# The upper diagonal blocks of the first attention pass: mask by a bf16 matmul in the bank, four block maxima in one VectorE operation

## The reference

```python
content = einsum('bqhd,bkhd->bhqk', q + u_bias, k)
pos_score = _rel_shift(einsum('bqhd,khd->bhqk', q + v_bias, p))
attn = softmax((content + pos_score) / sqrt(128), axis=-1)
x = x + (attn @ v) @ Wo + bo
# router: layernorm, hidden layer, top 2 of 8 experts
for e in range(8):
    output += expert_mask[e] * ((x1 * gelu(x2)) @ W2[e] + b2[e])   # x1, x2 = split(x @ W1[e])
```

## Time and profile before

| | |
|---|---|
| median of 3 runs | 1679.14 us (1678.62 to 1680.92) |
| span of the profiled execution | 1679.0 us |
| loop over batches, about | 87 to 1232 us of the span |
| expert phase, about | 1313 us to the end |
| TensorE matmul busy, all | 1548.0 us, 92% |
| VectorE busy, all | 1397.8 us, 83% |
| ScalarE busy, all | 1108.9 us, 66% |
| GpSimd busy, all | 1103.0 us, 66% |

### The profile page before, as it was taken

The page is one execution under the profiler, slowest core; times in us unless marked ns, Lnnn a source line. Parts: engine busy times, 40 slices in busy tenths (PEclk is TensorE's granted clock), DMA queues, the critical chain, the costliest instruction groups (busy, mean ns, idle before and its releaser), DMA issues. The chain is left out here.

```text
span 1679.0 us, 50905 instructions
## 1 busy us (share of the span) xinstructions
PE 1548.0 (92%) x12492; PEld 1204.6 (72%) x12493; DVE 1397.8 (83%) x5262; ACT 1108.9 (66%) x2295; POOL 1103.0 (66%) x2088
## 2 busy tenths in 40 slices
PE   3789999999999999999999999999952699999997
PEld 1567776677777767777777776776741699999997
DVE  4669899989989987998998899899864588887886
ACT  2157777776777776677777777767730477777775
POOL 5247767767766775777677677667673276666665
PEclk8679999999999998999999999999985799999999
DMA  5746535535644553464365355346454244444443
GB/s 136 198 116 174 148 93 152 164 96 128 180 116 128 161 148 84 110 203 110 104 174 148 93 141 164 97 129 179 122 153 136 42 58 54 56 56 52 56 53 49
DMA packets 133844, 199.72 MB, mean 119 GB/s; under 512 B 20888, under 2 KB 95016, under 8 KB 133632
## 3 DMA queue, kind: packets, MB, share of 16 engines
q1 hardware_dynamic: 108064, 177.07, 39.0%
q0 software_dynamic: 25568, 20.14, 8.2%
HBM read 108.10 MB, written 75.20 MB: 109 GB/s over the span
## 5 line engine op out<-in xcount | busy, mean ns | idle before, releaser
L1084 DVE CUSTOM_DVE_ANT_0 junk<-pA,lmask 128x512 bf16<-128x512 f32 x1056 | 686.9, 683 | 65.1 <-PE pA L671 45.9
L986 ACT ACTIVATE prob<-pB 128x512 f32<-128x512 f32 x384 | 229.8, 598 | 205.5 <-PE pB L690 115.9
L1578 POOL DMA_INDIRECT out<-yb,dst x142 | 230.4, 1622 | 131.3 <-ACT yb L1656 78.5
L692 PE MATMUL pB<-QL,K 97*128 97x512 f32 (+3 forms) x768 | 286.4, 373 | 1.4 <-ACT upper_diag L986 1.2
L669 PE MATMUL pA<-K,QL 96*128 96x512 f32 (+3 forms) x792 | 282.1, 357 | 5.1 <-DMA K<-split_operands 3.4
L690 PE MATMUL pB<-QU,K 97*128 97x512 f32 (+3 forms) x640 | 267.5, 418 | 0.2
L671 PE MATMUL pA<-K,QU 96*128 96x512 f32 (+3 forms) x660 | 233.1, 354 | 4.4 <-DVE acc L1084 3.2
L988 ACT ACTIVATE prob<-pB 128x512 f32<-128x512 f32 x384 | 227.9, 594 | 12.7 <-PE pB L692 3.4
L708 PE MATMUL pC<-prob,vext 128*17 128x256 f32 x3088 | 217.8, 385 | 0.1
L576 POOL TENSOR_TENSOR prob<-prob,upper_diag 128x128 f32<-128x128 f32 x384 | 179.7, 468 | 31.9
L690 PEld LDWEIGHTS pB<-QU,K 97*128 97x128 f32 x640 | 122.0, 191 | 99.9 <-issue 62.3
(11 more groups left out here) (305 smaller groups left out, 3642.9 us busy)
## 6 DMA issues: line engine op xcount, KB each, us to landing
QL<-split_operands SPq DMA_DIRECT2D x67, 256.0 KB
QU<-split_operands SPq DMA_DIRECT2D x67, 256.0 KB
K<-split_operands SPq DMA_DIRECT2D x67, 256.0 KB
xg<-routed_rows SPq DMA_DIRECT2D x75, 132.0 KB
split_operands<-c_h SPq DMA_DIRECT2D x36, 256.0 KB, 6.1
split_operands<-c_l SPq DMA_DIRECT2D x36, 256.0 KB, 6.4
QL<-split_operands SPq DMA_DIRECT2D x67, 128.0 KB
QU<-split_operands SPq DMA_DIRECT2D x67, 128.0 KB
```

What stands on the lines that cost most here:

```text
L692: mm = pe.matmul(pB[:, q0 + up:q0 + HALF], K[0:r, s, k], QL[0:r, s, q0 + up:q0 + HALF], start=True, stop=True)
L986: act.activation(p[:, 0:HALF], pB[:, 0:HALF], ACT.Exp, scale=SCALE).then_inc(p_exp, 1)
L1084: v.tensor_tensor_reduce(out, src[:, :], lmask[:, at:at + HALF], 1.0, -3.0e38, ALU.add, ALU.max, acc[:, s, qb, n % 2:n % 2 + 1]).then_inc( ...
L1578: po.indirect_dma_start(dram["out"], bass.IndirectOffsetOnAxis(dst[k][:, a:a + 1], 0), yb[k][:, a, :], None, compute_op=ALU.add).then_inc( ...
```

## The change

The mask of the upper diagonal pieces goes into the bank by one more matmul, ahead of the four: bf16 identity (stationary) times the bf16 mask, read four times by a stride of 0, 512 columns. The four score matmuls then add to the bank (`start=False`). VectorE takes the four block maxima with one `tensor_reduce` over 128 x 4 x 128. `umask` becomes bf16, and GpSimd sets up a bf16 identity `ident_b` (one memset and one select more). The registers of GpSimd in the expert phase are loaded with the runtime check of their bounds, which was skipped before.

```diff
-        lmask, umask = sb("lmask", [P, 15 * P], BF16), sb("umask", [P, P])
+        lmask, umask, ident_b = sb("lmask", [P, 15 * P], BF16), sb("umask", [P, P], BF16), sb("ident_b", [P, P], BF16)
-        DVE_SET, DVE_BIAS, POOL_SET = 13, 11, 15
+        DVE_SET, DVE_BIAS, POOL_SET = 13, 11, 17
             po.memset(umask[:, :], 0.0).then_inc(set_pool, 1)
+            po.memset(ident_b[:, :], 0.0).then_inc(set_pool, 1)
...
-            po.wait_ge(set_pool, 9)
+            po.wait_ge(set_pool, 10)
             po.affine_select(out=ident[:, :], in_=ident[:, :], compare_op=ALU.not_equal, fill=1.0, base=0,
                              pattern=[[-1, P]], channel_multiplier=1).then_inc(set_pool, 1)
+
+            po.affine_select(out=ident_b[:, :], in_=ident_b[:, :], compare_op=ALU.not_equal, fill=1.0, base=0,
+                             pattern=[[-1, P]], channel_multiplier=1).then_inc(set_pool, 1)
...
                 else:
+                    pe.matmul(dst[:, :].rearrange("p (n k) -> p n k", k=P), ident_b[:, :], umask[:, :].unsqueeze(1).to_broadcast([P, 4, P]),
+                              start=True, stop=False, skip_group_check=True)
                     for i in range(4):
                         q = slice(P * (4 * (n % 2) + i), P * (4 * (n % 2) + i) + P)
-                        mm = pe.matmul(dst[:, P * i:P * i + P], QU[0:KROWS, s, q], K[0:KROWS, s, q], start=True, stop=True)
+                        mm = pe.matmul(dst[:, P * i:P * i + P], QU[0:KROWS, s, q], K[0:KROWS, s, q], start=False, stop=True, skip_group_check=True)
...
                     g = n % 2
-                    for i in range(4):
-                        blk = 4 * g + i
-                        ttr = v.tensor_tensor_reduce(out[:, P * i:P * i + P], src[:, P * i:P * i + P], umask[:, :], 1.0, -3.0e38, ALU.add, ALU.max,
-                                                     acc[:, s, blk, 2:3])
-                    ttr.then_inc(s1_read, 1)
+                    v.tensor_reduce(acc[:, s, 4 * g:4 * g + 4, 2], src[:, :].rearrange("p (n k) -> p n k", k=P), AX.X, ALU.max).then_inc(s1_read, 1)
...
                     step.after = nc.values_load_multi_w_load_instructions(
-                        keep["add_after"][0:1, bass.ds(it * TURNS, TURNS)], engines=(mybir.EngineType.Pool,), min_val=1, max_val=TILES * ADD_N,
-                        skip_runtime_bounds_check_because="at least one addition, at most all")[1]
+                        keep["add_after"][0:1, bass.ds(it * TURNS, TURNS)], engines=(mybir.EngineType.Pool,), min_val=1, max_val=TILES * ADD_N)[1]
```

## The result

| | before | after |
|---|---|---|
| time, us: median (range) | 1678.88 (1678.25 to 1680.92) | 1704.77 (1703.70 to 1710.88) |
| span of the profiled execution, us | 1679.0 | 1702.7 |
| ratio to before, 95% interval | | 1.0139 (1.0112 to 1.0166) |

The change makes the kernel 25.9 us slower. The forecast was slower by 10.7 us; the time lies at the rival "TensorE leads everywhere" (1706).

The account below looks back on a forecast made before the run. TensorE was taken to bound most of the loop, VectorE only some stretches. The terms 14.1 + 0 - 2.5 - 0.9 = 10.7 us, put on the median 1679.1, gave 1690.0 us (+0.65%), range 1673 to 1708.

Parts of the forecast that it names:

- TensorE leads everywhere: Rival: all 128 masks in the loop lie in full on the path, 27 us more, 1706 us; chance 0.18.
- TensorE, added: One 512-column mask matmul at each diagonal piece costs TensorE 0.22 us (bounds 0.11 and 0.42), 28.2 us in the loop.
- VectorE, removed and added: At each diagonal piece one reduce of 0.63 us replaces four operations of 0.85 us, saving 0.22 us, 28 us in the loop.
- How the two meet: Loop's diagonal pieces: eight a batch where VectorE waits cost 14.1 us, the others about 0, GpSimd's waits give back 2.5.
- 7 of 16 pieces: Diagonal pieces of a batch whose bank is full before VectorE comes: sum about 0, bounds 12.3 us either way.
- 2.5 us in my favour: TensorE's waits for GpSimd's masked blocks, partly behind the diagonal piece at u = 4, take up 2.5 us (bounds 0 and 9).
- gain of 0.9 us ahead of the loop: VectorE leads at the four diagonal pieces ahead of the loop, each saving 0.22 us, 0.9 us in all.
- The checks: GpSimd's register bounds checks in the expert phase cost nothing, as their queue waits 78.5 us for ScalarE.
- The clock: Loop stretches at TensorE's lower clock level may go or come: 8 us either way, of which nothing was expected.
- VectorE leads: Rival: VectorE's chain through heads 1, 3, 6 and 7 sets the batch's pace, so faster, 1666 us; chance 0.12.
- The two cancel: Rival: waits for exps and GpSimd take up the eight pieces' delay, within 3 us, 1679 us; chance 0.16.
- the mask costs 0.42 us: Rival: each mask matmul at a diagonal piece takes 0.42 us, another 26 us of TensorE time, 1703 to 1715 us; chance 0.06.

Follow-up runs that it names:

- TensorE's part alone: After, but the four blocks overwrite the mask matmul's result and VectorE adds the mask in its four operations as before: 1701.68 us, ratio 1.0115.
- five operations: Before, with one more VectorE operation at each diagonal piece, a maximum over 128 columns that nobody reads: 1693.01 us, ratio 1.0056.
- the kernel with the moved code: After, with 140 tiny VectorE writes added ahead of the loop to shift its code: 1700.25 us, ratio 1.0111.
- VectorE's part alone: Before, with one reduce in place of VectorE's four operations and no mask anywhere, TensorE as before: 1684.48 us, ratio 1.0010.
- before with the checks: Before, with only the runtime check of GpSimd's register bounds in the expert phase added: 1686.47 us, ratio 1.0017.
- two blocks: Before, with only two of the four TensorE blocks of each diagonal piece computed, VectorE's work unchanged: 1655.84 us, ratio 0.9836.

## Why the prediction was wrong

*What bounds the kernel: right, and then not followed.* The reading was that TensorE is the bound over most of the loop, by the waits of the other engines for it. That is what the runs show.

*TensorE, added: right.* 0.22 us was taken, 0.18 and 0.23 measured between neighbours; in the length of the batch one mask is worth 0.18 us (2.9 / 16, TensorE's part alone). The bounds 0.11 and 0.42 are both ruled out. The 131 ns that the Trainium skill ("TensorE: Matmul & The Clock Gate", Back-to-back issue gap) gives as the sustained spacing, 16.8 us in all, are too low here.

*VectorE, removed and added: right.* 0.63 us was taken for the reduce; its record is 691 ns and it holds the next for 0.61 us. The four groups cost nothing on top.

*How the two meet: here it failed, twice.* First, 7 of 16 pieces were counted at about nothing, since the bank is full before VectorE comes to it. A full bank says that VectorE is late at that moment, not that its lateness reaches TensorE: there are three banks (`pA`) between them, and VectorE catches up at the next wait. One needs to see TensorE wait for VectorE, and that was 8.5 us for banks and 10.7 us for the router's results in the whole loop. The five operations measured it: of 3.2 us more on VectorE in a batch, 0.4 reach the batch. In the sizes that were measured the 16 pieces come to 8 x (2.9 - 0.4) = 20 us, where this step, with the 2.5 us for GpSimd, had 14.1 + 0 - 2.5 = 11.6. That is 8.4 of the 15.2 us that are missing, within the 12.3 that the step itself gave the seven pieces as a bound. Head 1, for which a gain of 0.2 us was forecast because VectorE has no idle time in it, became 0.4 us longer, as long as with the mask and no relief at all (16.71 in TensorE's part alone); head 3 not shorter but 0.1 longer. Only heads 2 and 3 took up their masks nearly whole (+0.02 and +0.10).

Second, the 2.5 us in my favour from waits for GpSimd, and the gain of 0.9 us ahead of the loop, did not come (there about 1 us was lost, by the kernel with the moved code). TensorE's short waits for exps and masked blocks grew with the change, from 23.3 to 26.7 and from 14.0 to 15.1 us, so they took nothing up. The likely reason is that they are made by TensorE's own earlier results, which ScalarE and GpSimd wait for, and so move along with it; no run tests that.

*VectorE's loop got shorter: not in the sum.* The change takes 7 instructions away from VectorE at each piece and so moves its code; the branch back to the loop's start then costs 1.0 us more there, 0.5 us of the batch (144.5 less 144.0) and 3.5 us for seven branches back. Nothing in the trace of before shows this price, but the branch itself is there.

*The sum again, with what was measured:* 8 x (2.9 for TensorE - 0.4 for VectorE's relief) + 7 x 0.5 for its branch = 23.5 us, and about 1 us ahead of the loop, against 25.9. The 1.4 us that are left have no cause that was shown; the interval of the result is 4.5 us wide to either side.

*The checks:* nothing, as forecast. *The clock:* 8 us either way was said. In the two profiles the stretches in the loop took 6.3 us off, and 10 us more at the lower level go with most of the 4.6 us that were added ahead of it. In runs that were not profiled the stretches are not known one by one.

*The rivals.* "TensorE leads everywhere" had the right place and a price of 27 us, and it was given 0.18. That its 1706 us is so near is in part luck: a mask is worth 0.18 us of a batch and not 0.22, some of the relief does count, and VectorE's branch, which was in no sum, fills part of that up. Its own argument, that the other engines wait for TensorE for over 190 and 75 us, was the stronger one: what was set against it were a few short waits of TensorE. "VectorE leads" is refuted by VectorE's part alone: it gained 0.5 us of a batch in heads 0 to 6, where 1.5 were needed, and nothing in the time. "The two cancel" and "the mask costs 0.42 us" fall with the batch's 3.0 us and the 0.18 to 0.23.

## What to carry to other kernels

Work moved from a busy engine to the one that sets the pace is paid in full, and the relief of the other is worth at most what that engine made the first one wait for (here some 20 us of a loop of 1100, of which 3 came back). Ask for each place who waits for whom, and take "no idle time in a stretch" as a sign of a burst that buffers even out, not of a lead. A test in both directions is cheap: add a small operation to each engine in turn at the place in question; the one that stretches the period leads. And when instructions are added to or taken from a loop that is thousands of instructions long, look at the branch back on each engine before and after.

## What the runs showed of the hardware

The branch back to the start of a long loop can cost an engine very different times for the same body of work: VectorE 0.46 us or 1.4 to 1.7 us, put right by 140 instructions ahead of the loop; TensorE nothing that shows with up to 24 masks in the batch, and 3.1 to 3.8 us with 32, which a shift by 216 instructions did not put right. Why 32 and not 24, and whether another shift would do, stays open.

This standstill of TensorE was followed by 6.8 us at the lower clock at each of the seven branches back of the two kernels that have it. Otherwise the loops have stretches at 1.2 GHz of 3.4 us, which cost 1.5 us each, and now and then one of 6.8 or 13.7 us (3.1 and 6.3 us), most of them in head 5 of a batch and in unequal number: none to three in the profiles of the five kernels that have the mask once or one and a half times, two and one in before and before with the checks, and five to seven in those with VectorE's part alone, five operations or two blocks. They alone can move the time of a kernel by some 10 us. What sets their number stays open.

A bf16 mask matmul of 512 columns between f32 ones costs 0.16 to 0.23 us, no more than an f32 one of that width (0.23), and the change of type shows no cost of its own.
